# Recommender tower: three groups looked up from padded tables at the start, transposes two groups at a time later

## The reference

```python
e = jnp.stack([tbl_f[ids[:, f]] for f in range(32)], axis=1)   # 1024 x 32 x 64
p, q = e[:, ROW], e[:, COL]                                    # 496 pairs, ROW < COL
kp = jnp.einsum('bpj,ipj->bpi', p, kernel)
z = jnp.sum(kp * q, axis=-1)
h = jnp.concatenate([z, dense_ctx], axis=1)                    # 1024 x 512
h = jnp.maximum(h @ W_top1 + b_top1, 0.0)                      # 512
h = jnp.maximum(h @ W_top2 + b_top2, 0.0)                      # 256
y = h @ W_top3                                                 # 1
```

## Time and profile before

| | us |
|---|---|
| median of three runs | 451.44 (450.06 to 451.81) |
| profiled execution, its own time | 451.3 |
| its span | 449.5 |
| TensorE busy (PE) | 428.2, 95% |
| VectorE busy (DVE) | 302.9, 67% |
| GpSimd busy (POOL) | 230.5, 51% |
| ScalarE busy (ACT) | 70.5, 16% |
| granted TensorE clock, mean | 0.996 of full speed |

### The profile page before, as it was taken

One profiled execution on the slowest core, in us unless ns is written; L12 is line 12 of the kernel. 1 busy time (PEld: TensorE's weight loads), 2 busy tenths in 40 slices (PEclk: granted clock), 3 DMA queues, 4 the chain that ended last, 5 costly groups with the idle time before them and its releaser, 6 DMA issues.

```text
span 449.5 us, 10096 instructions
## 1 busy us (share of the span) xinstructions
PE 428.2 (95%) x4290; PEld 283.0 (63%) x4290; DVE 302.9 (67%) x324; ACT 70.5 (16%) x154; POOL 230.5 (51%) x248
## 2 busy tenths in 40 slices
PE   0769999999999999999999999999999999999997
PEld 0447666767676766767676676767676766664442
DVE  4466687786878686886788787877887787860000
ACT  1002211102021111011221110111211201101122
POOL 4775776556576656565767574747674300000000
PEclk9989999999999999999999999999999999999999
DMA  5663444342111111110111110111151000000000
GB/s 141 199 192 80 126 123 125 100 131 62 22 40 39 25 33 25 20 41 18 39 36 30 29 28 19 39 23 37 31 177 33 14 1 14 1 1 1 0 0 0
DMA packets 15316, 23.55 MB, mean 52 GB/s; under 512 B 5505, under 2 KB 7809, under 8 KB 15144
## 3 DMA queue, kind: packets, MB, share of 16 engines
q1 hardware_dynamic: 6884, 14.14, 10.4%
q0 software_dynamic: 7808, 8.01, 9.3%
q10 hardware_dynamic: 580, 0.76, 0.6%
HBM read 20.79 MB, written 0.00 MB: 46 GB/s over the span
## 4 chain that ended last, share of the span: by engine, by line
PE 95%; DMA 3%; issue 1%; ACT 0%; SPq 0%
PE kp L535 52%; PE z_ps L552 25%; PE kp L573 6%; PE tr_ps L519 5%; PE tr_ps L511 3%; PE kp L579 3%; DMA k_sb<-in_tbl 3%; PE kp L586 0%; ACT pair L393 0%; ACT prod L437 0%; SPq L332 0%; SPq L338 0%; SPq L341 0%
## 5 line engine op out<-in xcount | busy, mean ns | idle before, releaser
L481 DVE TENSOR_TENSOR prod<-kp,pair 128x1024 f32<-128x1024 f32 x224 | 259.0, 1216 | 83.9 <-PE kp L535 83.9
L375 POOL DMA_INDIRECT raw<-in_tbl,ids_sb x244 | 230.3, 944 | 122.1 <-issue 67.0
L535 PE MATMUL kp<-pair,k_sb 64*128 64x256 f32 x1984 | 238.8, 387 | 0.0
L535 PEld LDWEIGHTS kp<-pair,k_sb 64*128 64x128 f32 x1984 | 182.9, 187 | 41.9 <-DVE prod L481 11.3
L552 PE MATMUL z_ps<-prod,ones_sel 128*32 128x256 f32 x1984 | 117.0, 382 | 0.0
L552 PEld LDWEIGHTS z_ps<-prod,ones_sel 128*32 128x32 f32 x1984 | 59.7, 110 | 50.5 <-issue 10.7
L393 ACT ACTIVATE pair<-tr_ps 128x256 f32<-128x256 f32 x64 | 24.5, 383 | 247.4 <-PE tr_ps L519 218.6
L511 PE MATMUL tr_ps<-prod,k_sb 125*64 125x256 f32 x96 | 14.3, 464 | 17.9 <-DMA k_sb<-in_tbl 13.4
L491 DVE TENSOR_TENSOR prod<-kp,pair 128x512 f32<-128x512 f32 x48 | 30.0, 681 | 0.0
L573 PE MATMUL kp<-z_sb,k_sb 128*128 128x512 f32 x64 | 28.0, 596 | 0.0
L519 PEld LDWEIGHTS tr_ps<-ident,raw 128*128 128x128 f32 x122 | 12.3, 141 | 24.2 <-issue 23.3
(11 more groups left out here) (9 smaller groups left out, 7.4 us busy)
## 6 DMA issues: line engine op xcount, KB each, us to landing
k_sb<-in_kd SPq DMA_DIRECT2D x15, 512.0 KB, 4.1
raw<-in_tbl,ids_sb POOLq DMA_INDIRECT x244
pair<-pair SPq DMA_DIRECT2D x32, 64.0 KB, 2.3
k_sb<-in_tbl SPq DMA_DIRECT2D x6, 250.0 KB
k_sb<-in_w SPq DMA_DIRECT2D x1, 1024.0 KB
hot_ids_sb<-in_hot_ids SPq DMA_DIRECT2D x3, 250.0 KB
z_sb<-in_dense ACTq DMA_DIRECT2D x1, 512.0 KB, 8.8
k_sb<-in_w SPq DMA_DIRECT2D x1, 512.0 KB
```

The lines of the kernel that those rows point to most:

```text
L375: nc.gpsimd.indirect_dma_start(raw[:, r % RAW_RING, i, n, :], None, tables[f], bass.IndirectOffsetOnAxis(ap=ids_sb[:, 2 * b + i, f:f + 1], ...
L481: nc.vector.tensor_tensor(prod[:, u % PROD_RING, :, :].rearrange("p q (i n) -> p (q i) n", i=UNIT_SLOTS), kp[u % KP_RING][:, :, :].rearran ...
L535: last = nc.tensor.matmul(kp[u % KP_RING][:, q, i * WIDTH:(i + 1) * WIDTH], k_sb[rows, x, :], pair[rows, group_place(st, owner // 2), :], ...
```

## The change

The first three groups (0, 1, 2) are now the looked-up ones, all at unit 0. Their six tables are put, on the host, into one array `small` padded to 1024 rows: 128 partitions by 8 rows, one DMA of 512 KB a lookup. Ids are broadcast to 128 partitions, both fields in one row of 512, and a compare covers both (8 of 512 columns a lookup). SP loads ids and tables of all three first, then slots 0 to 3 of the pair kernel, waits for all tables, and goes on with slots 4 to 15; the first load of 8 slots is split in two. The second event's result goes to `z_ps`, so that it need not wait for the first one's copy.

The row numbers and the ids of the first 256 samples come first on ScalarE's queue, the other ids after the constants; the dense inputs are loaded at unit 24. TensorE waits for no constants at first: it runs nine matmuls on zeros (`WARM`), into a `kp` buffer that is overwritten later.

From the second stage on an event brings two groups: four transposes, one copy of 512 columns, and both `raw` buffers come free at once. `TRANSPOSE_AT` is set for 16 + 24 events.

```diff
-STAGES = (1, 1, 1, 1)
+STAGES = (1, 2, 2, 2)
...
-LOOKUP = (0, 2, 4)
-SMALL = 1000
-SMALL_P, SMALL_C = 125, 8
+LOOKUP = (0, 1, 2)
+SMALL, SMALL_C = 1000, 8
...
+WARM = 9
+DENSE_AT = 24
...
-TRANSPOSE_AT = [0, 0, 0, 1, 2, 3, 7, 9, 13, 15, 20, 23, 25, 31, 36, 41, 43, 47, 52, 57, 61, 62, 66, 71, 74, 77, 82,
-                87, 90, 93, 98, 103, 105, 109, 114, 119, 123, 124, 128, 133, 136, 139, 144, 149, 152, 155, 160, 165,
-                167, 171, 176, 181, 185, 186, 190, 195, 198, 201, 206, 211, 214, 217, 222, 227]
+TRANSPOSE_AT = [0, 0, 0, 1, 2, 4, 7, 10, 13, 16, 20, 23, 28, 31, 36, 41, 43, 52, 57, 66, 71, 82, 87, 98, 103, 114,
+                119, 128, 133, 144, 149, 160, 165, 176, 181, 190, 195, 206, 211, 222]
...
-        def hot(i, n, c):
-            at = (SMALL_C * n + c) * WIDTH
-            return prod[0:SMALL_P, HOT_UNITS * i + at // (2 * ROWS), at // ROWS % 2, at % ROWS:at % ROWS + WIDTH]
+        def hot(i, c):
+            return prod[:, HOT_UNITS * i + c // 2, c % 2, :]
...
-        K_LOADS = [(j, min(j + K_LOAD, SLOTS)) for j in range(0, SLOTS, K_LOAD)]
+        K_LOADS = [(0, K_LOAD // 2), (K_LOAD // 2, K_LOAD)]
+        K_LOADS += [(j, min(j + K_LOAD, SLOTS)) for j in range(K_LOAD, SLOTS, K_LOAD)]
+        K_LOAD_AT = {first: j for j, (first, end) in enumerate(K_LOADS)}
...
+        ids_rest_in = sem("ids_rest_in")
+        zeros_ready = sem("zeros_ready")
...
+        def event_ps(e):
+            return z_ps if e == 1 else tr_ps
...
-                sp.dma_start(hot_ids_sb[0:SMALL_P, i, :, :],
-                             hot_ids[i:i + 1, :, :].broadcast_to([SMALL_P, 2, WIDTH])).then_inc(hot_ids_in[i], 16)
+                sp.dma_start(hot_ids_sb[:, i, :],
+                             hot_ids[i:i + 1, :].broadcast_to([P, 2 * WIDTH])).then_inc(hot_ids_in[i], 16)
...
-                for n in range(2):
-                    table = tables[2 * LOOKUP[i] + n].rearrange("(p c) e -> p c e", c=SMALL_C)
-                    sp.dma_start(table_sb[0:SMALL_P, i, n, :, :], table).then_inc(table_in[i], 16)
-            load_hot_ids(0)
-            sp.dma_start(row_sb[0:SMALL_P, :], row_no).then_inc(row_no_in, 16)
-            load_tables(0)
-            load_hot_ids(1)
-            load_tables(1)
+                sp.dma_start(table_sb[:, i, :, :, :], small[:, i, :, :, :]).then_inc(table_in[i], 16)
+            for i in range(len(LOOKUP)):
+                load_hot_ids(i)
+                load_tables(i)
...
-            load_hot_ids(2)
-            load_tables(2)
+            for i in range(len(LOOKUP)):
+                sp.wait_ge(table_in[i], 16)
...
                     mix_across(st, m)
-                j = s // K_LOAD
-                if st == 0 and s % K_LOAD == 0 and j + K_AHEAD < len(K_LOADS):
+                if u == DENSE_AT:
...
-                    load_k(j + K_AHEAD)
+                    sp.dma_start(z_sb[:, FC - 1, :], dense).then_inc(dense_in, 16)
+                if st == 0 and s in K_LOAD_AT and K_LOAD_AT[s] + K_AHEAD < len(K_LOADS):
+                    sp.wait_ge(kp_done, u + 1)
+                    load_k(K_LOAD_AT[s] + K_AHEAD)
...
         def _(pool):
+            nc.gpsimd.memset(z_sb[:, 0, 0:WIDTH], 0.0).then_inc(zeros_ready, 1)
...
+                if b and not GATHER[r - 1][1]:
+                    pool.wait_ge(ids_rest_in, 16)
...
         def _(act):
-            act.dma_start(ids_sb[:, :, :], ids).then_inc(ids_in, 16)
+            act.dma_start(row_sb[:, :], row_no).then_inc(row_no_in, 16)
+            act.dma_start(ids_sb[:, 0:WIDTH // P, :], ids[:, 0:WIDTH // P, :]).then_inc(ids_in, 16)
...
-            act.dma_start(z_sb[:, FC - 1, :], dense).then_inc(dense_in, 16)
+            act.dma_start(ids_sb[:, WIDTH // P:, :], ids[:, WIDTH // P:, :]).then_inc(ids_rest_in, 16)
...
                 st, k, n, raws = EVENT[e]
...
-                                     tr_ps[:, 0:n * WIDTH].rearrange("p (n w) -> p n w", n=n),
+                                     event_ps(e)[:, 0:n * WIDTH].rearrange("p (n w) -> p n w", n=n),
...
-                    for n in range(2):
-                        nc.vector.tensor_scalar(hot(i, n, c), hot_ids_sb[0:SMALL_P, i, n, :],
-                                                row_sb[0:SMALL_P, c:c + 1], None,
-                                                ALU.is_equal).then_inc(hot_ready, 1)
+                    nc.vector.tensor_scalar(hot(i, c), hot_ids_sb[:, i, :], row_sb[:, c:c + 1], None,
+                                            ALU.is_equal).then_inc(hot_ready, 1)
...
         def _(pe):
-            pe.wait_ge(consts_in, 2 * 16)
+            pe.wait_ge(zeros_ready, 1)
+            for i in range(WARM):
+                nc.tensor.matmul(kp[KP_RING - 1][:, 1, 0:WIDTH], z_sb[:, 0, 0:P], z_sb[:, 0, 0:WIDTH],
+                                 start=True, stop=True)
...
                 st, k, n, raws = EVENT[e]
-                if e:
-                    pe.wait_ge(evacuated, e)
+                if e > 1:
+                    pe.wait_ge(evacuated, e if e > 2 else 1)
...
-                    pe.wait_ge(table_in[lookup], 2 * 16)
+                    pe.wait_ge(table_in[lookup], 16)
...
+                        pe.wait_ge(hot_ready, SMALL_C * lookup + c + 1)
...
-                            pe.wait_ge(hot_ready, 2 * (SMALL_C * lookup + c) + i + 1)
-                            last = nc.tensor.matmul(tr_ps[64 * i:64 * i + 64, 0:WIDTH],
-                                                    table_sb[0:SMALL_P, lookup, i, c, :], hot(lookup, i, c),
+                            last = nc.tensor.matmul(event_ps(e)[64 * i:64 * i + 64, 0:WIDTH], table_sb[:, lookup, i, c, :],
+                                                    hot(lookup, c)[:, i * WIDTH:(i + 1) * WIDTH],
...
+                    if r == 0:
+                        pe.wait_ge(consts_in, 2 * 16)
...
-                        last = nc.tensor.transpose(tr_ps[:, to:to + P],
+                        last = nc.tensor.transpose(event_ps(e)[:, to:to + P],
...
-                    if st == 0 and x % K_LOAD == 0:
-                        pe.wait_ge(k_in[x // K_LOAD], 16)
+                    if st == 0 and x in K_LOAD_AT:
+                        pe.wait_ge(k_in[K_LOAD_AT[x]], 16)
...
     tables = [tables[f] for f in field_at]
+    small = _np.zeros((2 * len(LOOKUP), P * SMALL_C, EMBED), _np.float32)
+    for i in range(len(LOOKUP)):
+        for n in range(2):
+            small[2 * i + n, 0:SMALL] = tables[2 * LOOKUP[i] + n]
+    small = small.reshape(len(LOOKUP), 2, P, SMALL_C, EMBED).transpose(2, 0, 1, 3, 4)
...
-    hot_ids = _np.stack([ids_in[0:WIDTH, 2 * k:2 * k + 2].transpose(1, 0) for k in LOOKUP])
-    row_no = _np.arange(SMALL, dtype=_np.float32).reshape(SMALL_P, SMALL_C)
+    hot_ids = _np.stack([ids_in[0:WIDTH, 2 * k:2 * k + 2].transpose(1, 0).reshape(-1) for k in LOOKUP])
+    row_no = _np.arange(P * SMALL_C, dtype=_np.float32).reshape(P, SMALL_C)
```

More of the change, by code:

```diff
@@ L229, in dense_row, with pairwise_tower @@
     return 32 * (n // (32 - used)) + used + n % (32 - used)
-def pairwise_tower(nc, dense, ids, hot_ids, row_no, tables, kd, ident_in, sel_in, w1, b1, w2, b2, w3, out):
+def pairwise_tower(nc, dense, ids, hot_ids, row_no, small, tables, kd, ident_in, sel_in, w1, b1, w2, b2, w3, out):
     from contextlib import ExitStack
@@ L248, in pairwise_tower @@
         w3_sb = sb("w3_sb", [P, N2, 32])
-        hot_ids_sb = sb("hot_ids_sb", [P, len(LOOKUP), 2, WIDTH], I32)
+        hot_ids_sb = sb("hot_ids_sb", [P, len(LOOKUP), 2 * WIDTH], I32)
         row_sb = sb("row_sb", [P, SMALL_C])
@@ L654 @@
     sel[64:128, 31] = 1.0
-    arrays = {"dense": dense_rows, "ids": ids, "hot_ids": hot_ids, "row_no": row_no, "ident": _np.eye(P, dtype=_np.float32), "sel": sel}
+    arrays = {"dense": dense_rows, "ids": ids, "hot_ids": hot_ids, "row_no": row_no, "small": small, "ident": _np.eye(P, dtype=_np.float32), "sel": sel}
     for f in range(FIELDS):
@@ L666 @@
     out = nc.dram_tensor("out_y", (HALVES, ROWS), _mybir.dt.float32, kind="ExternalOutput").ap()
-    pairwise_tower(nc, ap["dense"], ap["ids"], ap["hot_ids"], ap["row_no"], [ap[f"tbl_{f}"] for f in range(FIELDS)], ap["kd"],
+    pairwise_tower(nc, ap["dense"], ap["ids"], ap["hot_ids"], ap["row_no"], ap["small"], [ap[f"tbl_{f}"] for f in range(FIELDS)], ap["kd"],
                    ap["ident"], ap["sel"], ap["w1"], ap["b1"], ap["w2"], ap["b2"], ap["w3"], out)
```

## The result

The changed kernel takes 444.26 us (median of 6 runs, 443.87 to 447.72) against 451.50 (6 runs) of the kernel before, measured with it: ratio 0.9854, 95% interval 0.982 to 0.9888. It is faster by 7.2 us where 14.9 were forecast; 444.26 lies above the range of 434.3 to 442. The profiled execution took 444.4 us, its span is 442.5.

What follows compares the result with a forecast made beforehand. The prediction saw a 43 us start bound by loads, then a body bound by TensorE's own sequence. From 451.3 us it took 12.9 for the start and 1.9 for the body, giving 436.5, range 434.3 to 442.

Steps and rivals of the forecast that it cites:

- The gathers are the next late thing: Start, POOL: gathers every 1.25 us from about 4.1, group 6's last ending at 23.9, a wait of 0.5 us.
- only lets POOL start sooner: Start, ids: the smaller first id load was to do nothing but start POOL earlier; gathers from about 4.1 us.
- rival D: Start, lookups: TensorE stays at 1.2 GHz through them, 10 us later, 446 us in all; chance 0.03.
- Rival C: First stage: gathers late at units 7, 13, 43, each costing 1 to 2 us; 438.5 to 440 us; chance 0.08.
- The compares: Start, VectorE: first at 4.2 us, 4.85 us a lookup, width setting the price without fixed part, end 18.7.
- The lookups: Start, TensorE: its chunks follow the compares, ending one chunk and one switch behind them, at 19.4 us.
- Rival B: Start: loads stay the bound, last table at 21.3 us; 442 us in all, half way 439.5; chance 0.14.
- the warm-up, priced at nothing: Start, TensorE: nine matmuls on zeros, over at 5 to 9 us, counted as neither gain nor loss.
- 10.2 us of units and events: First stage: units 0 to 8 (8.75 us) plus four events of 0.37 us before the first reduction.
- The body: Between reductions: fewer events save 6.6 us, moved events 0.55, added transposes cost 5.3; net 1.9 us less, 354.1.
- keeps up in the body: Body, POOL: gathered rows arrive in time, tightest at unit 43, which holds by 1.6 us.
- Rival E: Body: POOL sets the pace if a gather exceeds 1.45 us; at 1.6 us the time is 464; chance 0.02.

Runs made afterwards that it cites:

- ids_first: Changed kernel with ids ahead of the row numbers on ScalarE's queue, SP's loads not held back; 589.48 us, ratio 1.1188 on a slower chip.
- ids_alone_2: Changed kernel, first ids ahead of row numbers and SP's tables held back until ids landed; 440.78 us, 0.9758 (first run, slower chip: 585.14 us, 1.1105).
- five_engines: Changed kernel with the lookups' ids and tables loaded, compared and multiplied on 125 partitions, padding undone; 445.77 us, ratio 0.9861.
- direct_rows_2: Changed kernel, first four gathered groups read by SP as consecutive table rows, without lookup by ids; 436.79 us, 0.9705 (first run, slower chip: 579.04 us).
- body_only_2: Kernel before with only events of two groups in stages 2 to 4; 449.51 us, 0.9964 (first run, slower chip: 587.73 us, 1.1175).
- fill_2: Changed kernel with 7 and 5 matmuls on zeros before TensorE's waits at units 2 and 7; 445.93 us, 0.9856 (first run, slower chip: 587.0 us).
- k_load4_3: Kernel of ids_alone_2 with kernel slots loaded four at a time, first loads two; 439.55 us, 0.9751 (earlier runs, slower chips: 587.48, 586.0 us).
- start_only: Changed kernel with events of one group in stages 2 to 4 as before; 531.01 us (1.0055) and 531.34 us (1.003), both on slower chips.
- after: The profiled execution of the changed kernel itself, nothing further changed; 444.4 us.
- warm0: Changed kernel without the nine warm-up matmuls on zeros; 589.96 us, ratio 1.1192 on a slower chip.

## Why the prediction was wrong, point by point

**The step that failed** is "The gathers are the next late thing": POOL from about 4.1, one gather every 1.25 us, group 6's last ended at 23.9, a wait of 0.5. Measured: POOL from 7.42, one gather of 3.26 us among the first four, group 6's last ended at 30.29, waits of 2.98 and 2.15 us with a fall of the clock behind each. Its parts:

- The ids. I wrote that the smaller id load "only lets POOL start sooner". It landed at 7.15, later than the whole id load of before (4.66), with the row numbers ahead of it in its queue and seven loads of 256 and 512 KB that SP issues by 3.95 beside it. Put first in its queue it lands at 5.71 (`ids_first`), with SP held back as well at 4.28 (`ids_alone_2`). I had counted the queues one by one and given each load its landing time from another neighbourhood.
- The gathers. The price of 0.94 + 0.30 was right for every gather behind the compares, also at a DMA share of 0.91. Beside the block of wide compares the first four take 1.20, 1.23, 1.28 and 3.26 us. I had counted the compares only as work of VectorE and never asked what they do to POOL. In the trace before, three blocks of narrow ones with pauses between had cost POOL nothing. The eighth gather ended at 20.29 where my pace from 4.1 gives 13.8. Of the 6.5 us, 3.3 are the late start and 3.2 the slow gathers (0.26, 0.29, 0.34 and 2.32 over 0.94); POOL never made it good before unit 7.
- Landing. I allowed 3 to 4 us for group 6's last. It took 4.05 (29.34 to 33.40, chain above), of which 0.94 is the gather. Right in size. But that gather itself ended 6.4 us later than forecast (30.29 against 23.9).
- The clock. I had priced its fall only in rival D, for the lookups. It fell behind the wait at unit 2 and behind that at unit 7, for 3.4 us each, and work at 1.2 GHz is worth half: about 1.7 us each. The second reached into the stretch behind the first reduction (9.26 us instead of 8.82).

In sum from the first product to the first reduction: 10.2 by the forecast, 2.98 and 2.15 of waits, 1.7 for the first fall and 1.2 for what of the second lies ahead of 36.98, together 18.2; measured are 18.3 (36.98 - 18.70). Rival C named this mechanism and gave it 0.08 and at most 3.5 us. It named unit 7 and not unit 2, and had the size wrong, since it took each gather at its undisturbed price and had no fall of the clock. The range ends at 442 for the same reason.

**The compares** were mis-sized, in the kernel's favour. 24 compares of 512 columns take 9.59 us, 3.20 a lookup, where I took 4.85. From the starts of neighbouring compares, 0.262 us with 256 columns in the trace before and 0.397 with 512 after, an instruction has a part of about 0.13 us that doesn't grow with its width (an estimate from these two). I had read "no fixed part" from a product of another kind of operands, and my 0.306 us was a price beside gathers: in the block with POOL idle a compare costs 0.27. The first compare started at 5.59 and not at 4.2: it waits for the row numbers, which land 4.8 us after their issue, and the first ids too took 4.6 us where I took 3.4. The rule of the Trainium skill that I dismissed (VectorE: DVE Perf Modes, section "The TRN2 errata": 58 cycles per instruction from SBUF, 0.060 us) was nearer in kind, and half as large as what shows here.

**The lookups** therefore weren't bound by compares. TensorE took 3.5 us each from 8.19 on, when the warm-up ended, and the first product came at 18.70, 0.7 before the forecast of 19.4: two errors that nearly cancel. Tables were there at 6.97, 9.39 and 11.63, better than the 13.5 forecast for the last. Rival B didn't happen, and the warm-up, priced at nothing, is worth under 1 us.

**From there to the first reduction** 10.2 us of units and events is right: `five_engines` has 10.25 with nothing in the way, and `direct_rows_2` has 11.73 (18.13 to 29.86) with the wait of 1.41 us for slots in it. That `direct_rows_2` meets 30.1 so closely is in part luck: a first product 1.3 us early, no wait of 0.5, and those 1.41 us late.

**The body** came out by its own steps. From one reduction to the next, a stretch with an event of two at its run's head takes 7.61 us instead of 7.39, the 0.22 of the forecast; one that loses its head event goes from 7.82 to 7.45. In all 354.66 to 354.74 in the runs without disturbance, 1.2 to 1.3 us less than before, 355.08 in the changed kernel. The forecast of 354.1 was 0.5 too good: the event of unit 9, moved into a run, made that stretch 8.82 instead of 8.62, where I had it gain 0.28. The stretch with units 71 to 76 is 9.13 instead of 8.61 in every kernel with the new first stage and 8.77 in `body_only_2`; why was not tried.

**POOL** keeps up in the body even from 7.42 on: no wait for rows behind unit 7. Rival E's price of 1.45 us per gather was passed for four gathers at the start, and never for a stage.

## What to carry to other kernels

When a change makes one stage quicker, ask what will now be late: here the rows came hardly later than with loads of 125 partitions, but TensorE was there first. Price an instruction beside what runs at the same time on other engines: a block of wide compares on VectorE can hold a gather of GpSimd to its end, so look at where a long instruction ends, and what else ends there, before you put it down to DMA traffic. Load what starts the longest chain first, and hold the large loads back until it has landed: ids first in their queue and one wait on SP's gave 3.5 us here. To a wait of TensorE add the loss of clock that may stand behind it (1.6 to 1.7 us here), but mend first what it waits for.

## What the runs showed of the chip beyond this

- A gather of 0.94 us took up to 8.01 us (`ids_first`), 4.84 (`fill_2`) and 3.65 (`k_load4_3`) beside 16 or 24 compares of 512 columns in a row, and ended 0.11 to 0.13 us after the last of them. Which one is hit differs from execution to execution; in both of `start_only` and two of `k_load4` none was, and gathers beside compares took up to 1.28.
- The clock fell behind waits of 2.15, 2.23, 2.98 and 3.38 us, in `five_engines` behind 2.32 and 2.43, and not behind one of 2.5 (`k_load4_3`, unit 4) nor the shorter ones; each of these falls lasted 3.4 us.
- From the end of a group's last gather to the event that waited for it there were 2.1 to 4.0 us in `after`, `ids_alone_2`, `fill_2` and `k_load4_3`, all with slot loads moving, and 1.6 to 1.7 in `warm0`, `ids_alone` and `ids_first` with few. No run changes that alone.
- On three of the five chips that the experiments fell on, TensorE stood idle for 0.8 to 7.4 us at a time (the longest in `fill`, before 33.78), in places that no wait in the profile explains. The products' reduction in `ids_alone` on such a chip, then in `ids_alone_2`, the same kernel on the other (columns as in the earlier trace rows, with shapes):

```profile
L572 PE MATMUL z_ps<-prod,ones_sel 128*32 128x256 f32 x1984 | 180.6, 397 | 52.2 <-issue 48.7
```

```profile
L572 PE MATMUL z_ps<-prod,ones_sel 128*32 128x256 f32 x1984 | 117.0, 381 | 0.0
```

  48.7 us of idle are put down to issue on the one and none on the other. There every kernel with events of two that computes everything was 11 to 12% slower than the kernel before (585 to 590 us against 527 to 529), and those with events of one were not (531.01 and 531.34), while on the other chips events of two are a gain. `direct_rows` was 579.04. What in the order of instructions decides that is open; it was not tried.
